# Four residual layers on one core: output copies, bound and quarter units in a new order around the scan, scan rows loaded in two parts

## What is computed

```
x = x + L0(gn(x));  x = x + L1(gn(x));  x = x + L2(gn(x));  x = x + L3(gn(x))

def L1(x):
    x_ssm, res, gate = split(silu(in_proj_w @ x + b), 3)      # 3 x 512 channels
    xf = silu(depthwise_conv_3(x_ssm) + dw_b)                  # 512 x 1024
    dt, B_t, C_t = split(dbc_w @ xf + dbc_b)                   # for each head 1, 8 and 8 rows; dt = softplus
    x_h, dt, B_t, C_t = (gather(v, perm[head]) for v in ...)   # tokens into the head's order
    for t in range(1024):                                      # state h: 256 x 8 for each head
        h = exp(dt_t * A) * h + dt_t * B_t * x_t
        y_t = h @ C_t + D * x_t
    y = gather(y, inverse perm) * silu(gate) + res
    return silu(out_proj_w @ y + b)
```

## Time and profile before

| | us |
|---|---|
| median of three runs | 1747.64 |
| lowest, highest | 1746.6, 1761.05 |
| the profiled execution | 1750.19 |
| its span, first to last instruction | 1748.4 |

### The profile page before, as it was taken

How to read it: one execution, slowest core, us unless ns; L and a number is a source line. 1 busy time by engine, 2 the same in 40 slices (tenths; PEclk the granted TensorE clock), 3 DMA queues, 4 the chain that set the end, 5 groups by cost and what they waited for, 6 DMA issues and landing times.

```text
span 1748.4 us, 24401 instructions
## 1 busy us (share of the span) xinstructions
PE 1651.4 (94%) x8693; PEld 927.0 (53%) x8693; DVE 1147.0 (66%) x2472; ACT 892.9 (51%) x1091; POOL 413.1 (24%) x423
## 2 busy tenths in 40 slices
PE   4689899999999999999999999999999999999988
PEld 3254554555545655456545565455554565545643
DVE  6878776557855676647865568565775576662775
ACT  4647353565355654455634645356525555445542
POOL 0304311044021331133220341204402142113220
PEclk9889999999999999999999999999999999999999
DMA  6203410134102331223211341023410233112301
GB/s 207 94 0 103 145 28 13 73 127 145 40 25 89 114 118 40 74 92 105 95 21 73 127 139 34 14 85 120 140 40 36 84 117 109 40 48 75 102 25 49
DMA packets 124078, 140.16 MB, mean 80 GB/s; under 512 B 52259, under 2 KB 101475, under 8 KB 123950
## 3 DMA queue, kind: packets, MB, share of 16 engines
q1 hardware_dynamic: 109902, 103.18, 18.6%
q0 software_dynamic: 12288, 34.68, 5.9%
q10 hardware_dynamic: 1760, 0.64, 0.2%
HBM read 78.46 MB, written 60.01 MB: 79 GB/s over the span
## 4 chain that ended last, share of the span: by engine, by line
PE 64%; DVE 10%; issue 9%; POOL 9%; DMA 4%; ACT 3%; SPq 0%; DVEq 0%; POOLq 0%; ACTq 0%
PE bank L1618 61%; POOL d_scan L463 6%; DMA rows<-d_y,rank 1%; POOL rows L480 1%; DVE bn L913 1%; DMA d_y<-buf_b 1%; PE bank L1786 1%; POOL work L469 1%; DVE gate L1136 1%; PE bank L1917 1%; PE bank L1837 1%; DVE res L1260 1%; DVE res L1258 1%; DMA rows<-d_scan 1%; ACT res L643 1%
## 5 line engine op out<-in xcount | busy, mean ns | idle before, releaser
L1618 PE MATMUL bank<-buf_a,win_hi 128*128 128x512 f16 x1536 | 461.9, 383 | 8.2 <-DVE buf_a L985 8.1
L1618 PE MATMUL bank<-buf_a,win_lo 128*128 128x512 f16 x768 | 293.6, 382 | 0.0
L1618 PE MATMUL bank<-buf_b,w_hi 128*128 128x512 f16 x960 | 288.1, 382 | 2.3 <-DVE buf_b L985 2.3
L1618 PEld LDWEIGHTS bank<-buf_a,win_hi 128*128 128x128 f16 x1536 | 149.5, 99 | 174.5 <-DVE buf_a L985 10.9
L463 POOL DMA_INDIRECT d_scan<-rows,rank x128 | 125.3, 979 | 347.3 <-ACT rows L648 304.7
L1618 PE MATMUL bank<-buf_b,w_lo 128*128 128x512 f16 x480 | 183.2, 382 | 0.0
L1618 PE MATMUL bank<-buf_a,w_hi 128*128 128x512 f16 x576 | 171.3, 379 | 1.4 <-DVE x_odd L1228 1.3
L1618 PEld LDWEIGHTS bank<-buf_b,w_hi 128*128 128x128 f16 x960 | 94.0, 99 | 112.5 <-DVE buf_b L985 3.0
L480 POOL DMA_INDIRECT rows<-d_y,rank x128 | 125.8, 983 | 97.8 <-DMA d_y<-buf_b 61.6
L1618 PEld LDWEIGHTS bank<-buf_a,win_lo 128*128 128x128 f16 x768 | 75.7, 99 | 92.4 <-issue 3.0
L1618 PE MATMUL bank<-gate,w_out 128*128 128x512 f32 x256 | 120.2, 602 | 1.1 <-DVE gate L1341 1.1
(11 more groups left out here) (253 smaller groups left out, 3068.9 us busy)
## 6 DMA issues: line engine op xcount, KB each, us to landing
rows<-d_scan SPq DMA_DIRECT2D x16, 1092.0 KB, 5.8
d_y<-buf_b SPq DMA_DIRECT2D x64, 256.0 KB, 2.2
work<-in_x SPq DMA_DIRECT2D x24, 512.0 KB, 4.5
d_gram<-rows SPq DMA_DIRECT2D x32, 260.0 KB, 2.4
x_even<-in_x SPq DMA_DIRECT2D x16, 512.0 KB, 5.5
x_odd<-in_x SPq DMA_DIRECT2D x16, 512.0 KB, 5.4
out_x<-x_even SPq DMA_DIRECT2D x16, 512.0 KB, 3.1
out_x<-x_odd SPq DMA_DIRECT2D x16, 512.0 KB, 2.6
```

The costliest lines, as they stand in the source:

```text
L1618: return eng.matmul(out, lhsT, rhs, start=start, stop=stop, skip_group_check=True, **kw)
```

## The change

Five edits, in the programs of four engines:

- SP: a head's rows are loaded by two DMAs, the 17 columns of step size, B and C first (`scanrows`), then the 256 columns of x (a new semaphore, `scanx`), for which `state_products` waits at its first chunk.
- ACT: head 0's output copies stand each in front of an exponential of head 1, and no longer the first of them behind two exponentials. One of the three units between `scan_factors(1)` and the copies of head 1 goes behind `y_high(m, 0)`.
- DVE: `scan_states` of head 1 stands ahead of `y_largest`.
- TensorE, tokens: the quarter units around `tokens(3)` go from 4 and 20 to 5 and 19 (before the sum of the next image's statistics; the whole is the same).
- TensorE, scan of head 1: of the six quarter units ahead of its output product two are left, four go behind the four output chunks of head 0. The transpose of the bound goes into the output product ahead of chunk 6, the broadcast behind the first output chunk.

```diff
@@ SP
-                    eng.dma_start(rows4[:, h], d_scan[h].rearrange("(c p) r -> p c r", p=P)).then_inc(s[f"scanrows{h}"], 16)
+                    stored = d_scan[h].rearrange("(c p) r -> p c r", p=P)
+                    eng.dma_start(rows4[:, h, :, DH:ROW], stored[:, :, DH:ROW]).then_inc(s[f"scanrows{h}"], 16)
+                    eng.dma_start(rows4[:, h, :, 0:DH], stored[:, :, 0:DH]).then_inc(s[f"scanx{h}"], 16)
@@ ACT
                 scan_factors(0)
                 filler(2)
 
+                scan_y(0, 0)
                 scan_exp(1, 0)
+                scan_y(0, 1)
                 scan_exp(1, 1)
-                scan_y(0, 0)
+                scan_y(0, 2)
                 scan_exp(1, 2)
-                scan_y(0, 1)
                 scan_decays(1)
-                scan_y(0, 2)
                 scan_y(0, 3)
                 scan_factors(1)
-                filler(3)
+                filler(2)
                 for j in range(4):
                     scan_y(1, j)
                 y_high(m, 0)
+                filler(1)
                 y_high(m, 1)
                 filler(1)
@@ DVE
                 scan_blocks(m, 1)
+                scan_states(m, 1)
                 y_largest(m)
-                scan_states(m, 1)
                 y_scale(m)
@@ TensorE, tokens
                 tokens(2)
-                filler(1)
+                piece(KC + 1)
                 tokens(3)
-                filler(5)
+                piece(5 * KC - 1)
@@ TensorE, state_products
+                        if c == 0:
+                            wait(eng, f"scanx{h}", m, 16)
@@ TensorE, scan
+                def bound_across():
+
+                    wait(eng, "w_maxc", m, ROUNDS + 1)
+                    eng.transpose(bound_row, y_bound[:, 7:8], ident).then_inc(s["w_maxt"], 1)
+
-                def scan_y(h):
+                def scan_y(h, between=None):
 
                     r = rows4[:, h]
                     for c in range(NT):
+                        if c == NT - 2 and between:
+                            between()
@@ TensorE, behind scan_inner(1)
                 scan_inner(1)
-                wait(eng, "w_maxc", m, ROUNDS + 1)
-                eng.transpose(bound_row, y_bound[:, 7:8], ident).then_inc(s["w_maxt"], 1)
-                piece(6)
-                wait(eng, "w_maxr", m, 2 * ROUNDS + 3)
-                mm(bound_all, const("ones")[0:1, :], y_bound[0:1, 1:2], True, True).then_inc(s["w_maxb"], 1)
-                scan_y(1)
+                piece(2)
+                scan_y(1, bound_across)
@@ TensorE, output chunks
                 for n in range(4):
                     y_chunk(*gate_order[n])
-                piece(4)
+                    if n == 0:
+                        wait(eng, "w_maxr", m, 2 * ROUNDS + 3)
+                        mm(bound_all, const("ones")[0:1, :], y_bound[0:1, 1:2], True, True).then_inc(s["w_maxb"], 1)
+                piece(8)
```

More of the change, by code:

```diff
@@ L207, in build @@
             l0_done l0_evac l0_add_pool l0_add_dve in_done in_evac out_done out_evac out_add l2_done l2_add l3_done l3_add
-            conv_pad conv_mac conv_act tok_mm tok_ev dbc_mm sp_z sp_dve sp_act row_ready scattered0 scattered1 scanrows0 scanrows1
+            conv_pad conv_mac conv_act tok_mm tok_ev dbc_mm sp_z sp_dve sp_act row_ready scattered0 scattered1 scanrows0 scanrows1 scanx0 scanx1
             fac_mv fac_c fac_mm fac_arg fac_exp fac_gam fac_pq fac_8 fac_diag fac_tp fac_ptq mm_m m_ev dh_mm h_zero h_st y_mm y_ev y_out0 y_out1 y_in00 y_in01 y_in10 y_in11
@@ L218, in build @@
                    conv_pad=1, conv_mac=3 * KC, conv_act=KC, tok_mm=KC, tok_ev=KC, dbc_mm=1, sp_z=1,
-                   sp_dve=10, sp_act=2, row_ready=1, scattered0=16 * NT, scattered1=16 * NT, scanrows0=16, scanrows1=16,
+                   sp_dve=10, sp_act=2, row_ready=1, scattered0=16 * NT, scattered1=16 * NT, scanrows0=16, scanrows1=16, scanx0=16, scanx1=16,
                    fac_mv=3 * HEADS, fac_c=(T8 + 1) * HEADS, fac_mm=HEADS, fac_arg=3 * HEADS, fac_exp=3 * HEADS, fac_gam=HEADS, fac_pq=3 * HEADS,
```

## The result

| | before | changed |
|---|---|---|
| median of the runs, us | 1747.29 | 1779.39 |
| lowest, highest | 1746.6, 1761.05 | 1774.75, 1784.41 |
| span of the profiled execution | 1748.4 | 1777.0 |
| mean granted clock of TensorE | 0.984 | 0.973 |

The ratio is 1.0165 with a 95% interval of 1.0108 to 1.0222: the change makes the kernel slower by 1.7%, where I forecast 0.6% faster.

The account below looks back on a forecast made before the run. TensorE was taken as the bound, working 205.0 of 208 us of an inner image, so only idle time could be won. Terms of -3.2 - 12.2 - 9.2 - 1.0 + 14.2 = -11.4 us gave a median of 1736, range 1724 to 1749.

Parts of the forecast that it names:

- Step 1: Token step on TensorE: one quarter unit more ahead of it covers its last short wait, -3.2 us over the run.
- Step 2: Head 0's output copies on ACT: TensorE's wait on the first copy goes, -12.2 us; DVE's head 1 chain moves some -0.2.
- Step 3: Head 1's output product: moved units bring it 2.6 us forward, moved bound products 0.4; DVE's second sum has 0.2 us slack.
- the rival's costs: C's price for states missing head 1's output product by up to 0.5 us an image: +4.0 us.
- the sum: All terms over the run: -3.2 - 12.2 - 9.2 - 1.0 + 14.2 = -11.4 us.
- Step 4: Row load in two parts: the 17 columns land in 3 us (2.3 to 5.8); 0 us for TensorE.
- rival B: Head 0's gathers are ready, as early masks put DVE's head 1 chain 2 us ahead: no new wait, 1722 us; chance 0.21.
- Step 5: Head 0's gathered rows at the output chunks: TensorE comes sooner and waits 1.8 us an image, +14.2 us over the run.
- Step 6: Behind head 0's gathers: the wait for head 1's gathered rows goes, -9.2 us, and half that for its last copy, -1.0.
- C: Gathers 1.2 us late in every image and states late for the output product: whole gain given back, 1750 us; chance 0.12.
- D: The 68-byte part lands so late that masks hold up TensorE at the heads' sums: slower by over 1%; chance 0.04.
- E: Another wait stood behind that on head 0's first copy, so the copies change nothing: 1742 to 1747 us; chance 0.07.

Follow-up runs that it names:

- Experiment 2: The changed kernel with one small extra exponential ahead of ACT's first output copy, so that the exp table loads early: 1755.45 us, 1.0022 of the kernel before.
- experiment 1: The changed kernel with ACT's old order (two head 1 exponentials, then head 0's first copy): 1730.75 us, 0.9871 of the kernel before.
- experiment 11: The changed kernel with each head's rows in one DMA again: 1784.36 us, 1.0191 of the kernel before.
- experiment 3: The changed kernel with SP waiting for all eight head 0 gathers before issuing the next image's four loads: 1762.2 us, 1.0058 of the kernel before.
- experiment 9: The changed kernel with 20 unneeded products an image between the second and third output chunk: 1764.56 us, 1.0075 of the kernel before.

## Why the prediction was wrong, by its own steps

**Step 1** holds: the wait on the token step is down from 10.5 to 8.3 us, 2.2 where I gave 3.2. The first image's 7.9 us, of which I had counted 0.65 as won, did not move.

**Step 2** holds for TensorE (12.2 us gone) and fails for ACT. I worked out that exponential 0 starts when the copy ends, at 804.65; it starts 1.28 us later, behind the table load, which in the old order ran in ACT's idle time and had no price. So "DVE's chain moves by some -0.2 us" should have been +1.3. Experiment 2 shows the load's price, 1.4% in this schedule. And +1.3 is against the old kernel; against what the early columns would have given, the new order costs 3.5 us (11.5 against 8.0 in experiment 1).

**Step 3**: the 0.2 us of slack for the second sum was too little by that chain's delay (with the load out of the way, in experiment 2, the wait is gone); the miss was 0.6 us an image, 4.7 in all. I had put it among the rival's costs and 0 in the sum.

**Step 4**: the landing was 2.4 us, at the lower end of what I gave. From the rule of the Trainium skill that I had cited, "DMA: Bandwidth & Descriptors", *Specifications*, on transfers below 512 bytes, I had drawn that the small part may land no sooner than the whole row. The measurement decides against that reading: 2.4 us and not 5.8. It doesn't speak against the rule itself, which is about rate: 68 KB in 2.4 us is 29 GB/s, 1,092 KB in 5.8 us is 193. The step's 0 for TensorE is right within the change, 0 to 5 us by experiment 11, and hides the finding: alone the edit is worth 21 us. I followed the edits together and, apart from rival B, never asked what this one does on its own. That would have shown two cures for one wait, with the cheaper one enough.

**Step 5** names the right place and the wrong size: a wait at head 0's gathers of 1.8 us an image, measured 4.5. For the image shown I had 1.9 us, and it was 5.1. Three terms were off. The diagonal's delay from step 2 is +1.2 us (first gather 13.6 us behind the start of the output product, forecast 12.4). The landing is +3.1. I had taken it as 2.9 us from one row of head 1; in the old schedule the loads of the next image are issued 4.6 us behind the start of head 0's last gather, after the change 0.6 us (836.26 and 836.89). The loads had been moved by some 4 us along with TensorE, since SP waits for the output product, and I did not move them; they cost 2.1 us of the 3.1 in this image and 1.6 on the mean (experiment 3), and the cause of the rest is open. Against these, TensorE's lead is 1.2 us smaller: it comes to the chunk 23.4 us behind the start of head 0's product, 26.9 before, so 3.5 sooner and not 4.7; part of the difference is the new wait for DVE's sum. Together 1.9 + 1.2 + 3.1 - 1.2 = 5.0, with 5.1 measured.

**Step 6** holds: no wait for head 1's gathers nor for the last copy is left.

**The sum** counted waits only: -11.4 us forecast, +15.0 measured. It had no term for the clock, worth 13.7 us more in busy time than before (some 20 against the same kernel with the wait filled, experiment 9). In the kernel before, the longest wait of an inner image was 2.1 us, and the windows of the six inner images have a clock of 1.00 four times and 0.99 twice; after the change, with waits of up to 5.5 us, they have 0.98 five times and 0.99 once. "TensorE: Matmul & The Clock Gate" of the Trainium skill, Part 1, says that idle time throttles the engine to half rate. The trace agrees, with a clock of 0.56 behind the wait; the rule belonged with every forecast of a longer wait.

**The rivals**: it came out on C's side, beyond it, with C's place and with more than C's price. D, on which I put the whole of "slower", played no part. E was not it either, but its doubt was the right one: another edit did remove the wait on L727.

## What to carry to other kernels

When an instruction is moved ahead of an idle stretch's end, look for what else ran in that stretch unpriced, here a table load on ACT; and follow on every queue what starts by the moved engine's semaphores, here 2 MB of loads onto the last gathers. Price a new wait of the engine that bounds the kernel twice, as time and as the clock behind it; work that is put into the wait wins both. And take each edit of a bundle alone before taking them together: one of these five was worth 1.2%, and another, ACT's new order, which does nothing alone, hid it (0.9871 without that order, 1.0165 with it).

## What the runs showed of the hardware

- 1,024 runs of 68 bytes land in 2.4 us, as fast as the 640 of 20 bytes of each `d_gram` load (2.3), while 1,024 runs of 1,092 bytes take 5.8.
- A gather of 128 rows by GpSimd that starts 0.6 us ahead of four 512 KB loads from SP let TensorE go after 6.0 us, and after 3.9 with the loads held back. Over all images of all runs in which TensorE waited for head 0's last gather, it was 4.6 to 7.7 us where the loads were issued within 0.8 us of its start, and 3.2 to 5.5 where they came 1 us or more behind it or not at all.
- Waits of TensorE of 3.2 us an image (experiment 3) and 4.5 us (the changed kernel) came with mean clocks of 0.977 and 0.973, against 0.984 before; 20 unneeded products in the wait brought the mean clock from 0.973 to 0.987, and made the program some 15 us faster (0.9%).
- A load of ACT's table takes 1.28 us and runs ahead of the wait of the activation that it serves (799.21 in the kernel before, with the exponential at 804.84), but not ahead of an earlier copy in ACT's program (815.87).
